# Sums of a selective scan taken by accumulating transposes, tokens on partitions, and turned back in the second direction

## What is computed

```python
def step(h, inp):
    d_t, u_t, B_t, C_t = inp
    h = h * jnp.exp(d_t[..., None] * A) + (d_t * u_t)[..., None] * B_t[:, :, None, :]
    return (h, jnp.einsum('bkdn,bkn->bkd', h, C_t))
...
ys = ys + Ds[None, :, :, None] * xs
y0 = ys[:, 0] + ys[:, 2][..., ::-1]
y1 = ys[:, 1] + ys[:, 3][..., ::-1]
y1 = jnp.swapaxes(y1.reshape(B, -1, W, H), 2, 3).reshape(B, -1, L)
return y0 + y1
```

## Time and profile before

| | |
|---|---|
| median of 3 runs | 25830.78 us (25828.31 to 25838.94) |
| the profiled execution's own span | 25840.8 us |
| PE busy | 23779.6 us, 92% |
| DVE busy | 24469.9 us, 95% |
| ACT busy | 22148.9 us, 86% |
| POOL busy | 20751.4 us, 80% |
| mean granted clock of TensorE | 0.984 of 2.4 GHz |

### The profile page before, as it was taken

One profiled execution on the slowest core, in us unless ns is written; L12 is line 12 of the kernel. 1 busy time (PEld: TensorE's weight loads), 2 busy tenths in 40 slices (PEclk: granted clock), 3 DMA queues, 4 the chain that ended last, 5 costly groups with the idle time before them and its releaser, 6 DMA issues.

```text
span 25840.8 us, 379056 instructions
## 1 busy us (share of the span) xinstructions
PE 23779.6 (92%) x94368; PEld 13125.4 (51%) x94368; DVE 24469.9 (95%) x17461; ACT 22148.9 (86%) x49918; POOL 20751.4 (80%) x11892
## 2 busy tenths in 40 slices
PE   8999999999999999999989999999999999999998
PEld 4555555555555555555545555555555555555554
DVE  8999999999999999999989999999999999999999
ACT  8888988889888888889878898888888888988888
POOL 7777977788777977779768988888988888988888
PEclk9999999999999999999999999999999999999999
DMA  4444544445444544445444554444544444544444
GB/s 155 136 136 134 173 135 136 136 147 161 135 136 135 165 143 136 137 134 171 133 124 144 160 159 147 147 148 144 169 151 146 149 147 145 173 146 147 148 146 150
DMA packets 1419203, 3789.54 MB, mean 147 GB/s; under 512 B 205888, under 2 KB 206016, under 8 KB 1416384
## 3 DMA queue, kind: packets, MB, share of 16 engines
q1 hardware_dynamic: 1416768, 3762.72, 46.3%
HBM read 3686.39 MB, written 47.19 MB: 144 GB/s over the span
## 4 chain that ended last, share of the span: by engine, by line
PE 16%; issue 11%; ACT 10%; DVE 10%; POOL 3%; DMA 1%; DVEq 0%; ACTq 0%; SPq 0%; POOLq 0%
PE ps L830 6%; DVE arena L1537 5%; ACT arena L1274 4%; DVE ps L1532 4%; POOL arena L1674 2%; ACT arena L1209 2%; PE ps L1041 2%; PE ps L798 1%; PE ps L818 1%; DMA arena<-c_rows 1%; PE ps L667 1%; PE ps L652 1%; PE ps L836 0%; PE ps L835 0%; PE ps L840 0%
## 5 line engine op out<-in xcount | busy, mean ns | idle before, releaser
L1674 POOL TENSOR_TENSOR arena<-arena 128x768 f32<-128x768 f32 x9216 | 16583.8, 1828 | 1243.7 <-DVE arena L1537 925.0
L830 PE MATMUL ps<-arena,consts 128*128 128x384 f32 x36864 | 13640.3, 493 | 266.1 <-ACT arena L1308 224.3
L1537 DVE TENSOR_TENSOR_SCAN arena<-arena,carry,ps 128x768 f32<-128x768 f32 x6144 | 10903.6, 1805 | 191.5 <-PE ps L798 18.4
L1209 ACT ACTIVATE arena<-arena,An 128x768 f32<-128x768 f32 x9216 | 8491.5, 936 | 1516.3 <-POOL arena L1674 1511.8
L830 PEld LDWEIGHTS ps<-arena,consts 128*128 128x128 f32 x36864 | 6310.1, 191 | 3987.7 <-issue 444.3
L1532 DVE TENSOR_TENSOR ps<-ps,arena 128x768 f32<-128x768 f32 x5696 | 5377.3, 944 | 240.3 <-PE ps L818 235.4
L1537 DVE TENSOR_TENSOR_SCAN arena<-arena,ps 128x768 f32<-128x768 f32 x3072 | 5276.0, 1745 | 118.1 <-PE ps L798 44.1
L1274 ACT ACTIVATE arena<-arena 128x64 f32<-128x64 f32 (+1 forms) x13824 | 3921.3, 372 | 18.0
L1274 ACT ACTIVATE arena<-arena,bT 128x64 f32<-128x64 f32 (+1 forms) x12864 | 3646.3, 371 | 15.7
L798 PE MATMUL ps<-consts,arena 128*128 128x128 f32 x21120 | 2956.7, 276 | 729.2 <-DVE arena L1537 573.9
L798 PEld LDWEIGHTS ps<-consts,arena 128*128 128x128 f32 x21120 | 2415.1, 141 | 2314.4 <-issue 1331.6
(11 more groups left out here) (184 smaller groups left out, 19056.0 us busy)
## 6 DMA issues: line engine op xcount, KB each, us to landing
arena<-c_rows SPq DMA_DIRECT2D x6144, 384.0 KB, 3.8
arena<-c_rows SPq DMA_DIRECT2D x6144, 192.0 KB, 3.6
arena<-x SPq DMA_DIRECT2D x32, 864.0 KB, 6.8
arena<-arena SPq DMA_DIRECT2D x384, 72.0 KB, 2.5
arena<-mid SPq DMA_DIRECT2D x32, 864.0 KB, 6.7
c_rows<-arena SPq DMA_DIRECT2D x96, 192.0 KB, 3.1
mid<-arena SPq DMA_DIRECT2D x16, 864.0 KB, 3.9
out<-arena SPq DMA_DIRECT2D x16, 864.0 KB, 3.9
```

Source lines behind the costliest of these rows:

```text
L830: mm = pe.matmul(y_part[:, h, :], ident, hC[it % NH][:, h * SEG:(h + 1) * SEG], start=(n == 0), stop=(n == NS - 1))
L1209: act.activation(state_at[it % NW], delta[g % 2], ACT.Exp, scale=An[:, slot(s) * NS + n:slot(s) * NS + n + 1]).then_inc(sem["da_ready"], 1)
L1537: dve.tensor_tensor_scan(a[:, ::back], a[:, ::back], slots[it % 2][:, ::back], 0.0 if k == 0 else carry[:, n:n + 1], ALU.mult, ALU.add).th ...
L1674: pool.tensor_tensor(hC[it % NH], state_at[it % NW], Csb[b], ALU.mult).then_inc(sem["hc_ready"], 1)
```

## The change

For 17 of the 18 groups (`by_tokens`) the sum over states is taken by six transposes of 128x128 that accumulate in PSUM, in place of two matmuls with the identity. The sum then lies with tokens on partitions. `ysum` holds it so after p = 0, and after p = 1 as well. For the eight groups with p = 1 among them (`turned_back`: 3, 4, 5, 9, 10, 11, 15, 16) PE turns the sum back into `pre_part` at step 7 of the next group (`turn_back`), adds the inputs times D there, and for j = 0 also the inputs read by columns, which were added in groups 12 to 14 before; ACT copies the result to u[j] at step 9 (`keep_back`). Group 17 keeps the old adds and takes the other direction's sum by six transposes, and the inputs, at its step 12. The z units of groups 4 and 5 go to group 7, the third merge from group 10 to 13, and two of the turned columns come one and two steps later. What waited for the copy of sums and needs u[j] now waits for the copy back.

```diff
-COLUMNS_AT = {(2 * NC, 12): 2, (2 * NC + 1, 3): 1, (2 * NC + 1, 12): 0}
-FIRST_MERGE = 2 * NC + 2
-Z_IN = {2: (0, 1), 3: (2, 3), 4: (4,), 5: (5,)}
+COLUMNS_AT = {(2 * NC, 13): 2, (2 * NC + 1, 3): 1, (2 * NC + 1, 14): 0}
+MERGE_AT = (8, 9, 13)
+Z_IN = {2: (0, 1), 3: (2, 3), 7: (4, 5)}
...
+def by_tokens(g):
+    return g < NG - 1
+def turned_back(g):
+    return by_tokens(g) and group(g)[1] == 1
+def back_before(g):
+    return sum(turned_back(i) for i in range(g))
...
 STEP_AT = dict(pre=1, taken=5, exp=5, plus=6, log=7, less=7, lost=6, log1p=7, relu=9,
-               times=10, du=15, keep=1, sums=5, second=8, third=11, turn_b=11, keep_b=13, copy_c=9)
+               times=10, du=15, keep=1, sums=5, second=8, third=11, turn_b=11, keep_b=13, copy_c=9, back=7, kept=9)
...
# turn_du(g)
+                if g >= 2 and turned_back(g - 2):
+                    pe.wait_ge(sem["y_kept"], v("y_kept", back_before(g - 1)))
...
# add_state(it)
-                for h in range(2):
-                    mm = pe.matmul(y_part[:, h, :], ident, hC[it % NH][:, h * SEG:(h + 1) * SEG], start=(n == 0), stop=(n == NS - 1))
+                if by_tokens(g):
+                    mm = add_turned(y_part, hC[it % NH], n == 0, n == NS - 1)
+                else:
+                    for h in range(2):
+                        mm = pe.matmul(y_part[:, h, :], ident, hC[it % NH][:, h * SEG:(h + 1) * SEG], start=(n == 0), stop=(n == NS - 1))
                 mm.then_inc(sem["y_summed"], 1)
                 if p == 1 and n == 8:
-                    for h in range(2):
-                        at = c * CH + h * SEG
-                        pe.matmul(y_part[:, h, :], ident, ysum[:, at:at + SEG], start=False, stop=False)
-                        pe.matmul(y_part[:, h, :], diag_D[:, j, :], u[j][:, at:at + SEG], start=False, stop=False)
-                if p == 0 and j == 0 and n == 10:
-                    for h in range(2):
-                        r = (2 * c + h) * SEGROWS
-                        pe.matmul(y_part[:, h, :], ident, by_column(u[2])[:, r:r + SEGROWS, :], start=False, stop=False)
+                    if by_tokens(g):
+                        for h in range(2):
+                            at = c * CH + h * SEG
+                            pe.matmul(y_part[:, h, :], ident, ysum[:, at:at + SEG], start=False, stop=False, skip_group_check=True)
+                    else:
+                        add_turned(y_part, chunk(ysum, c), False, False)
+                        add_inputs(y_part, j, c)
+
+            def add_turned(to, src, first, last):
+                for i in range(TBL):
+                    h, at = i // 3, i % 3 * P
+                    mm = pe.matmul(to[:, h, at:at + P], src[:, i * P:(i + 1) * P], ident, is_transpose=True,
+                                   start=(first and at == 0), stop=last, skip_group_check=True)
+                return mm
+
+            def add_inputs(to, j, c):
+                for h in range(2):
+                    at, r = c * CH + h * SEG, (2 * c + h) * SEGROWS
+                    mm = pe.matmul(to[:, h, :], diag_D[:, j, :], u[j][:, at:at + SEG], start=False, stop=False, skip_group_check=True)
+                    if j == 0:
+                        mm = pe.matmul(to[:, h, :], ident, by_column(u[2])[:, r:r + SEGROWS, :], start=False, stop=False, skip_group_check=True)
+                return mm
+
+            def turn_back(g):
+                s, p, j, k, c = group(g)
+                if g + 2 < NG:
+                    pe.wait_ge(sem["pre_taken"], v("pre_taken", g + 3))
+                else:
+                    pe.wait_ge(sem["duT_ready"], v("duT_ready", NG))
+                pe.wait_ge(sem["y_moved"], v("y_moved", g + 1))
+                add_turned(pre_part, chunk(ysum, c), True, False)
+                add_inputs(pre_part, j, c).then_inc(sem["y_back"], 1)
...
# scan(g) of PE, between means_ahead and the z units
+                    if n == STEP_AT["back"] and g > 0 and turned_back(g - 1):
+                        turn_back(g - 1)
                     if n == STEP_AT["second"]:
                         if g in Z_IN:
                             in_proj_z(Z_IN[g][0], g)
-                        if 0 <= g - FIRST_MERGE < NC:
-                            merge_columns(g - FIRST_MERGE)
+                        if g in MERGE_AT:
+                            merge_columns(MERGE_AT.index(g))
...
# means_ahead(1) of PE; gate_sums of DVE has the same edit
-                    pe.wait_ge(sem["y_moved"], v("y_moved", NG - 1))
+                    pe.wait_ge(sem["y_kept"], v("y_kept", back_before(NG)))
...
# scan(g) of ACT, after the steps of delta, before copy_z
+                    if n == STEP_AT["kept"] and g > 0 and turned_back(g - 1):
+                        keep_back(g - 1)
...
-                act.copy(halves(chunk(ysum if p == 0 else u[j], c)), y_part).then_inc(sem["y_moved"], 1)
+                act.copy(halves(chunk(ysum if by_tokens(g) else u[j], c)), y_part).then_inc(sem["y_moved"], 1)
+
+            def keep_back(g):
+                s, p, j, k, c = group(g)
+                act.wait_ge(sem["y_back"], v("y_back", back_before(g + 1)))
+                act.copy(halves(chunk(u[j], c)), pre_part).then_inc(sem["y_kept"], 1)
 
             def turn_columns(c):
-                act.wait_ge(sem["y_moved"], v("y_moved", 2 * NC - c))
+                act.wait_ge(sem["y_kept"], v("y_kept", NC - c))
```

More of the change, by code:

```diff
@@ L111, with merged_before @@
 Z_UNITS = [(t, c) for t in range(2) for c in range(NC)]
-COLUMNS_AT = {(2 * NC, 12): 2, (2 * NC + 1, 3): 1, (2 * NC + 1, 12): 0}
-FIRST_MERGE = 2 * NC + 2
-Z_IN = {2: (0, 1), 3: (2, 3), 4: (4,), 5: (5,)}
+COLUMNS_AT = {(2 * NC, 13): 2, (2 * NC + 1, 3): 1, (2 * NC + 1, 14): 0}
+MERGE_AT = (8, 9, 13)
+Z_IN = {2: (0, 1), 3: (2, 3), 7: (4, 5)}
 C_PIECES = (6, 7)
+def merged_before(g):
+    return sum(i < g for i in MERGE_AT)
+def by_tokens(g):
[4 more added lines that the diff above has]
+    return sum(turned_back(i) for i in range(g))
 def z_before(g):
@@ L166 @@
     "duT_full": NG, "duT_ready": NG, "bT_full": PAIRS + 1, "bT_ready": PAIRS + 1, "scanned": NIT, "hc_ready": NIT, "y_summed": NIT,
-    "y_moved": (NG - 1, NG), "y_gated": (3, 0),
+    "y_moved": (NG - 1, NG), "y_gated": (3, 0), "y_back": back_before(NG), "y_kept": back_before(NG),
     "z_ready": len(Z_UNITS), "z_copied": len(Z_UNITS), "sz_ready": 2, "columns_turned": NC, "merge_ready": NC, "merge_taken": NC, "gated": (0, 6),
@@ L730, in merge_columns @@
                     pe.wait_ge(sem["columns_turned"], v("columns_turned", NC))
-                pe.wait_ge(sem["pre_taken"], v("pre_taken", FIRST_MERGE + c + 2))
+                pe.wait_ge(sem["pre_taken"], v("pre_taken", MERGE_AT[c] + 2))
                 hold(pe)
@@ L785, in turn_du @@
                     hold(pe)
-                if 0 <= g - 1 - FIRST_MERGE < NC:
-                    pe.wait_ge(sem["merge_taken"], v("merge_taken", g - FIRST_MERGE))
+                if g - 1 in MERGE_AT:
+                    pe.wait_ge(sem["merge_taken"], v("merge_taken", merged_before(g)))
+                    hold(pe)
+                if g >= 2 and turned_back(g - 2):
+                    pe.wait_ge(sem["y_kept"], v("y_kept", back_before(g - 1)))
                     hold(pe)
@@ L1238, in scan @@
                             copy_z(Z_IN[g][0])
-                        if 0 <= g - FIRST_MERGE < NC:
-                            move_merged(g - FIRST_MERGE)
+                        if g in MERGE_AT:
+                            move_merged(MERGE_AT.index(g))
                     if (g, n) in COLUMNS_AT:
@@ L1544, in gate_sums @@
                 dve.tensor_tensor(yg[1], yg[1], sz[1][0:DB, :], ALU.mult).then_inc(sem["y_gated"], 1)
-                dve.wait_ge(sem["y_moved"], v("y_moved", NG - 1))
+                dve.wait_ge(sem["y_kept"], v("y_kept", back_before(NG)))
                 dve.tensor_tensor(yg[0][:, CH:], yg[0][:, CH:], sz[0][:, CH:], ALU.mult).then_inc(sem["y_gated"], 1)
```

## The result

The changed kernel takes 25,985.75 us (median of 4 runs, 25,973.46 to 26,003.05) against 25,834.86 us for the kernel before (4 runs, 25,828.31 to 25,839.74). The ratio is 1.0058, with a 95% interval of 1.0046 to 1.0070: slower by 0.6%. The profiled execution took 25,991.0 us, 150 us more than that of before (25,840.8 us).

A forecast was written before the change was run, and what follows sets the result against it. The prediction took VectorE (DVE, busy 95%) as the bound. Per image -7.8 + 7.1 + 0.5 = -0.2 us at full clock; times 32 plus 112 us for low clock gave +106, so 25,935 us, range 25,660 to 26,150.

The forecast's parts named there:

- waits that go: DVE's waits for PE in the groups, 9.3 us an image, fall by 7.8, 250 us in all; group 7 keeps 1.5.
- bursts: New PE work in groups 16 and 17 makes DVE wait 6.1 us an image in layer 0, 8.1 in layer 1, mean 7.1.
- ACT: Eight more copies out of PSUM an image, 203 us in all, make DVE wait 0.5 us an image in groups 8 and 12.
- clock: PE's granted clock falls in thin plain steps, to 0.75 to 0.92 in the groups, costing 3.5 us an image, 112 in all.
- The adds: Six accumulating transposes hold PE 0.66 us where the old add held it 1.30; 5.6 ms less PE time.
- Rival 4: An accumulating transpose takes about as long as the old add (1.1 to 1.3 us): 26,110 us; chance 0.10.
- Rival 2: Faster: new work on PE in groups 16 and 17 is mostly covered, 5 us an image won: 25,660 us; chance 0.18.
- Step 0: Transposes of du behind a turned step 15, 12 groups, one in four at low clock, 0.5 lost each: 1.5 us an image.
- C rows and the last two groups: PE's C rows and the last two groups, at low clock, cost DVE 0.6 us an image together.
- Turned product 10: Made late by ACT's scaling, at low clock it costs 12 x 1/2 x 0.1 = 0.6 us an image.
- Rival 1: PE's clock holds, or its falls hit only covered work: 25,825 us, no difference; chance 0.19.
- Rival 3: Transposes don't hold the clock, so PE runs the groups at 1.2 GHz: about +2,500 us, 28,300; chance 0.04.

The follow-up runs named there:

- wide: The changed kernel with all by-token adds as f32 matmuls, not transposes, so each takes the old length; 26,090.10 us, 1.0095 of the kernel before.
- run 230: Not a label of a run: "Over the run 230 us for 227" gives waits summed over the changed kernel's whole profiled execution, 230 us measured, 227 forecast.
- nocol: The changed kernel without the inputs read by columns in groups 15 to 17, that part of the sum left out; 25,801.92 us, 0.9987 of the kernel before.
- spread: The changed kernel with inputs times D, column reads and layer 1's means moved to separate or later steps, results unchanged; 25,823.25 us, 0.9991 of the kernel before.
- half: The kernel before with the second half of most adds left out, no transposes and nothing turned back; 25,812.98 us, 0.9992 of the kernel before.
- half_held: The kernel before with the second half of most adds left out, plus two idle f32 matmuls in plain steps without extra work; 25,670.38 us, ratio 0.9934.
- held: The changed kernel plus two idle f32 matmuls of 128 columns in about half of the plain steps; 25,898.86 us, 1.0026 of the kernel before.
- held_turns: As held, but the idle work is four f32 transposes of 128x128 in place of two matmuls; 25,915.84 us, 1.0032 of the kernel before.

## Why the prediction was right, and by what it was off

Forecast 25,935, measured 25,986, in the range and on the side forecast. Against the profiled execution of before the forecast was +106 us, measured +150. The terms over the run, forecast and measured: waits that go -250 and -236, bursts +227 and +230, ACT +16 and next to nothing, clock +112 and +191, and -35 that had no term (DVE's own instructions and the stretches between images). So +80 us of misses stand against those -35: the total came out closer than its clock term.

- **The adds.** Right. Six accumulating transposes hold PE 0.67 to 0.69 us in the rows shown (3189.66 to 3190.35 turned back, 3194.20 to 3194.88 as an add), forecast 0.66. Rival 4 falls by these rows, and wide shows what it would have been.
- **Waits that go.** Forecast -250 us, measured -236 at full clock. Group 7, step 5, stays at 1.33 us in layer 0 and 1.66 in layer 1, mean 1.5 as forecast (before 2.24). That mean has luck in it: forecast were 1.0 at full clock and 2.0 at low, measured are 1.25 and 1.59.
- **Bursts.** Forecast 6.1 us an image in layer 0 and 8.1 in layer 1. Measured means: 1.75, 2.37 and 1.63, together 5.8, and in layer 1 1.75, 2.61, 2.10 and 2.15, together 8.6. Over the run 230 us for 227. Turning back in the other six groups is covered, as forecast: their step 8 waits 0.04 us, like any. nocol shows the cause, spread that it is the place and not the work. Rival 2 falls.
- **ACT.** Its copies cost 199 us for 203 forecast, but its busy time grew by 117 only, as its other instructions became a little shorter (exponentials 932 ns for 936, over 9,216). Of the forecast 0.5 us an image little shows: group 12, step 10, where I had 0.2, waits 0.11 us in the mean, and group 8, where I had 0.3, waits 0.23 at step 5, but for PE, in 14 images and with the low clock near (counted there). In all DVE waited 11.1 us for exponentials, before 12.2. These 12.2 us, 26 waits, also show that the sentence "it is never behind DVE" was wrong for the kernel before; the sum doesn't hang on it.
- **The clock.** The mechanism was right: half and half_held show it on their own, and held, though it gets back only part of it, is 83 us under the changed kernel. The size was off: 3.5 us an image forecast, 6.0 by the table (191 us, which sorts by the clock nearby). Step 0 came out right in the sum: forecast 1.5 with the transposes of du, measured 47.0 us, 1.5. But the count behind it was not: step 15 is turned in 16 groups, not 12, and 98 of the 109 waits fall in groups 9, 13, 14 and 15. C rows and the last two groups had 0.6. In groups 16 and 17 the clock was up in all 112 long waits. C rows of group 0 met the low clock in all 32 images; steps 7 and 8 waited 82 us there, where held has 31, so 1.6 an image. Merges weren't in the count: 10 of 96 met the low clock, at 3.8 us each, 1.2 an image. Nor was step 5 outside group 7 (30 us at low clock, 8 before). Turned product 10 had 0.6 and shows 0.1 (4.6 us at low clock), turning back had 0.8 and shows nothing. The upper bound failed as well: "at most 1.64 for one stretch of low clock" came from the one burst that the trace had at both levels, and a longer burst pays more; the merge paid 3.86. The merge lost 3.95 us on a burst of 4.68: nearly its own length again, as it had no slack.
- **What should show it.** PE busy: forecast 70 to 75%, measured 78%. The work that ran at half clock is part of it: an accumulating transpose averages 289 ns in the changed kernel and 279 in held. The clock in the groups is 0.94 (0.75 to 0.92 forecast), so the low clock was rarer and dearer than I had it. Waits moved where I said, and the merges' short waits at step 9 turned into few, long ones, in groups 9 and 13.
- **Rival 1** (the clock costs nothing) falls by held and half_held. **Rival 3** falls by half and held_turns.

How the clock comes to fall in one image and not in another at the same place (10 merges of 96) stays open; I made no run for it.

## What to carry to other kernels

Taking work off an engine that isn't the bound can pay only what the bound waits for it, and if that engine is TensorE it can lose its clock with it: look for the longest bursts that a low clock could meet, and price each with its own length again, less its slack. Keep the slow form of a piece of work where nothing waits, use the quick form ahead of a burst, and cut bursts over several steps: here that turned +0.6% into -0.4%, with the same change inside. When a sum is moved to a new layout, what has to be turned back or added at once in it is the cost, not the sum.

## What the runs showed of the hardware that I had not expected

- Once down, the clock stayed at 0.50 from about 9553 to 9563, while PE was busy without a gap: nearly a whole burst can run at half clock.
- Idle work on TensorE made the kernel faster: 0.58% in half_held against half and 0.32% in held against the changed kernel, with some 0.45 us more for PE in 92 steps an image (held).
- f32 transposes of 128x128 hold the clock just as f32 matmuls do (0.969 for both, 1,603 and 1,596 us low), and accumulate at the same 0.11 us from one to the next (0.68 for six) as those that don't (0.65 to 0.71).
